# Second attention's running sums in fp32r, bias products merged, a new slot table for all stages

## The chip, the cores and the metric

One core of one Trainium2 chip runs the whole program. The metric is device time in microseconds of one launch. Engines are named as the profile names them: PE (TensorE), DVE (VectorE), ACT (ScalarE), POOL (GpSimd), SP (SyncE, here only a DMA queue).

## The reference

The input x is 2048 tokens of 128 numbers (8 sequences of 256). Six stages are added to it in turn, each on a layer-normed x:

```python
x = x + 0.5 * L0_ffn(_layernorm(x))     # 8 experts, top 2, hidden 256
x = x + L0_attn(_layernorm(x))          # silu projections, relu^2 of q k^T, gate
x = x + 0.5 * L0_ffn(_layernorm(x))
x = x + 0.5 * L1_ffn(_layernorm(x))     # 8 experts, top 2, hidden 352
x = x + L1_attn(_layernorm(x))          # linear attention, 16 heads
x = x + 0.5 * L1_ffn(_layernorm(x))
```

Each expert layer normalises once more (RMS), picks two of eight experts per token, and adds down(up * silu(gate)) by weight. The second attention, with phi = elu + 1, F = 4 features and G = 8 values per head, is

```python
kv = cumsum(einsum('bhtf,bhtg->bhtfg', K, V), axis=t)
Z = 1 / (einsum('bhtf,bhtf->bht', Q, cumsum(K, axis=t)) + 1e-6)
out = einsum('bhtf,bhtfg->bhtg', Q, kv) * Z
```

All values are fp32.

## The kernel before, in words

The tokens are split into four batches b of 512 (two sequences, four tiles of 128). The four expert layers are steps s = 0 to 3. In each, the two rows per token are sorted by expert with a scatter to `rows_dram`, so that a batch makes at most 15 tiles of 128 rows with one expert each. Thus there are 60 tiles a step and 240 in all, and tile n is slot n of one clock that all engines share: in slot t PE does `up(t)` (four products of 128x128 in steps 0 and 1, six in steps 2 and 3), then `down(t-2)` (two or three), then the transposes of a round of rows where one is due, then the stages of the chains. ACT does the silu of tile t, DVE the product `mult(t)`, SP loads weights four slots ahead. Every engine writes out its own list, slot by slot, and runs it in order; the slot is therefore not a time but a place in five queues, and semaphores tie them.

A chain (s, b) is what leads from the end of batch b's tiles in step s to its tiles in step s+1: POOL gathers the results (`gather`, eight indirect DMAs, offsets 2 to 5), DVE adds them (`combine`, in halves), attention follows in the chains s = 0 and 2, then routing (`route`) and the scatter (eight indirect DMAs on POOL). The offset of a stage is counted in slots from the end of the batch's tiles. The tables `COMBINE`, `ATTENTION` (stages j = 3 to 15 or 3 to 21) and `ROUTE` hold the offsets by hand. Chains of successive batches are 15 slots apart, so in a long middle stretch every slot holds stages of up to three chains. Chains s = -1 route the input: they begin `LEAD` slots before the batch's tiles, and slots from -30 on run before the first tile.

What ties PE to DVE: `up` has three banks `up_gate`, of which steps 2 and 3 use two per tile, so gate(n) needs mult(n-2) (`bank_free`), as does down(n-2). PE's small products share bank side2 in a fixed order of turns (`claim`).

Second attention, batch by batch, in banks side0 and side1: stage 7 transposes; 8 and 9 the q, k, v products with a bias product each (`ones_b` 3 rows times the split bias, bf16); 9 to 12 phi on DVE and ACT; 13 to 16 POOL makes k times v of tile t (`R[3 + t]`, 128x512); 14 the running sum of k (`tri`, and `ones` for the second tile of a sequence); 15 to 18 the running sums of kv; 15 DVE the denominator; 16 to 19 DVE multiplies by q and reduces; 20 transposes; 21 output product and bias. First attention has its own stages 7 to 15 with bias products in 9, 10 and 15.

## Time and profile before

| | us |
|---|---|
| median of 3 runs (659.34, 665.21, 665.27) | 665.21 |
| profiled execution | 665.68 |
| its span, first to last instruction | 664.0 |
| PE busy in it | 591.2 |
| DVE busy | 432.1 |
| ACT busy | 236.5 |
| POOL busy | 277.3 |
| mean granted clock of PE | 0.976 |

The span is 1.68 us shorter than the execution. PE's busy time is the union of its matmuls, with ends that are modelled; its weight loads run beside them. A row with "x8" is eight instructions of one kind merged. Every fp32 matmul shows as two records.

### The profile page before, as it was taken

What the parts mean: (1) busy time and instruction counts of PE and PEld (TensorE: products, weight loads), DVE (VectorE), ACT (ScalarE), POOL (GpSimd) and SP (SyncE); (2) the same over time, 40 slices, a digit from 0 to 9 for tenths busy, and PEclk for the clock granted to TensorE, in tenths of its full rate; (3) what the DMA queues carried; (4) which work ended last, traced back from release to release, by engine and by line L of the source; (5) the groups of instructions that cost most, each with busy time, mean ns of one, the idle gap of its engine ahead of it and who ended that gap; (6) DMA issues with size and microseconds to landing.
All of it is one profiled execution on the core that took longest, in us unless ns stands there. A gap on an engine that the chain in (4) does not pass through costs nothing.

```text
span 664.0 us, 15563 instructions
## 1 busy us (share of the span) xinstructions
PE 591.2 (89%) x4600; PEld 538.2 (81%) x4600; DVE 432.1 (65%) x1628; ACT 236.5 (36%) x466; POOL 277.3 (42%) x327
## 2 busy tenths in 40 slices
PE   1289989999999997899999999999999999998960
PEld 1179877989889797888999988988888889898960
DVE  4676582776768568657667739669869769572321
ACT  1034434353443433333433352342342343332320
POOL 2452636045170634573727182065075074170413
PEclk9999989999999999989999999999999999998995
DMA  8478869566665557588979876656765766777831
GB/s 297 172 234 229 282 186 278 146 184 192 194 178 171 166 173 220 168 260 248 305 222 282 224 228 168 178 164 171 194 159 167 197 176 174 216 209 241 240 86 43
DMA packets 114405, 133.18 MB, mean 201 GB/s; under 512 B 10931, under 2 KB 77491, under 8 KB 114070
## 3 DMA queue, kind: packets, MB, share of 16 engines
q1 hardware_dynamic: 106134, 115.39, 59.5%
q0 software_dynamic: 8192, 16.79, 8.6%
q8 instruction: 42, 0.69, 0.4%
q14 instruction: 37, 0.30, 0.1%
HBM read 103.05 MB, written 29.10 MB: 199 GB/s over the span
## 4 chain that ended last, share of the span: by engine, by line
PE 68%; DVE 14%; issue 6%; DMA 5%; POOL 4%; ACT 2%; SPq 1%; POOLq 0%; DVEq 0%; ACTq 0%
PE up_gate L907 19%; PE up_gate L900 13%; PE y L861 12%; PE side L915 3%; PE y L863 3%; POOL y_rows L456 2%; PE side L982 2%; PE side L931 2%; POOL rows_dram L440 2%; DVE hidden L591 2%; PE side L990 1%; PE side L999 1%; DVE x_res L641 1%; PE side L966 1%; DVE attn_xT L803 1%
## 5 line engine op out<-in xcount | busy, mean ns | idle before, releaser
L456 POOL DMA_INDIRECT y_rows<-y_dram,rows_of x128 | 128.9, 1007 | 250.6 <-DMA y_dram<-y_tile 216.1
L591 DVE TENSOR_TENSOR hidden<-up_gate,hidden 128x256 f32<-128x256 f32 (+1 forms) x240 | 116.6, 488 | 119.5 <-PE up_gate L907 58.8
L501 ACT ACTIVATE hidden<-up_gate 128x256 f32<-128x256 f32 (+1 forms) x240 | 104.6, 436 | 247.7 <-PE up_gate L907 125.9
L907 PE MATMUL up_gate<-rows_T,up 128*128 128x128 f32 x1440 | 184.9, 278 | 0.6 <-ACT hidden L501 0.4
L907 PEld LDWEIGHTS up_gate<-rows_T,up 128*128 128x128 f32 x1440 | 172.5, 193 | 9.0 <-issue 6.5
L440 POOL DMA_INDIRECT rows_dram<-rms_out,rows_of x128 | 127.4, 995 | 119.7 <-DVE rows_of L729 83.0
L900 PE MATMUL up_gate<-rows_T,up 128*128 128x128 f32 x960 | 135.8, 287 | 5.3 <-issue 4.0
L900 PEld LDWEIGHTS up_gate<-rows_T,up 128*128 128x128 f32 x960 | 122.6, 199 | 14.4 <-issue 11.0
L861 PE MATMUL y<-down,hidden 128*128 x480 | 75.3, 280 | 2.4 <-DVE hidden L591 2.3
L861 PE MATMUL y<-down_a,hidden 128*128 x480 | 73.7, 276 | 0.0
L861 PEld LDWEIGHTS y<-down,hidden 128*128 128x128 f32 x480 | 64.9, 196 | 3.0 <-issue 3.0
L861 PEld LDWEIGHTS y<-down_a,hidden 128*128 128x128 f32 x480 | 63.7, 193 | 0.0
L506 ACT ACTIVATE rows_T<-side,norm 128x512 f32<-128x512 f32 x64 | 42.2, 660 | 52.0 <-PE side L915 52.0
L494 ACT ACTIVATE y_tile<-y 128x512 f32<-128x512 f32 x64 | 36.5, 570 | 32.8 <-PE y L863 29.8
L863 PE MATMUL y<-down_b,hidden 96*128 x240 | 46.5, 275 | 0.0
L915 PE MATMUL side<-ident,rows 128*128 128x128 f32 x240 | 38.2, 280 | 7.0 <-DMA rows<-rows_dram 5.8
L863 PEld LDWEIGHTS y<-down_b,hidden 96*128 96x128 f32 x240 | 36.6, 192 | 0.0
L915 PEld LDWEIGHTS side<-ident,rows 128*128 128x128 f32 x240 | 29.0, 145 | 8.1 <-DMA rows<-rows_dram 8.0
L641 DVE SCALAR_TENSOR_TENSOR x_res<-y_rows,w_first,x_res 128x128 f32<-128x128 f32 x64 | 19.7, 350 | 22.9 <-DMA y_rows<-y_dram,rows_of 22.6
L926 PE MATMUL side<-ident,rms_out 128*128 128x128 f32 x64 | 10.8, 296 | 19.9 <-DVE rms_out L627 18.7
L926 PEld LDWEIGHTS side<-ident,rms_out 128*128 128x128 f32 x64 | 8.0, 151 | 20.1 <-issue 10.9
L931 PEld LDWEIGHTS side<-router,z_T 128*128 128x128 f32 x128 | 17.2, 209 | 6.5 <-ACT z_T L513 6.5
(159 smaller groups left out, 629.9 us busy)
## 6 DMA issues: line engine op xcount, KB each, us to landing
up<-in_up SPq DMA_DIRECT2D x120, 352.0 KB
up<-in_up SPq DMA_DIRECT2D x120, 256.0 KB
rows<-rows_dram SPq DMA_DIRECT2D x48, 256.0 KB, 3.6
y_dram<-y_tile SPq DMA_DIRECT2D x48, 256.0 KB
rows_dram<-zeros SPq DMA_DIRECT2D x12, 256.0 KB, 4.5
rows<-rows_dram SPq DMA_DIRECT2D x16, 192.0 KB
y_dram<-y_tile SPq DMA_DIRECT2D x16, 192.0 KB
rows_dram<-rms_out,rows_of POOLq DMA_INDIRECT x128, 3.2
```

Of the source, the lines that this page charges most:

```text
L440: pool.indirect_dma_start(out=xg_d[g], out_offset=bass.IndirectOffsetOnAxis(ap=pos[g][:, at:at + 1], axis=0), in_=xs(Z, GROUPS[g][c // TB] ...
L456: pool.indirect_dma_start(out=gath[b % 2][:, (TB * k2 + c) * P:(TB * k2 + c + 1) * P], out_offset=None, in_=y_d[g], in_offset=bass.Indirec ...
L494: act.activation(ysb[r % 4][:, 0:n * P], Y[r % 2][:, 0:n * P], ACT.Copy).then_inc(y_done, 1)
L501: act.activation(hid[n % 4][:, 0:w], src, ACT.Silu).then_inc(silu_done, 1)
L506: act.activation(xgT[r % 3][:, 0:n * P], S[2][:, 0:n * P], ACT.Copy, scale=wn[:, LAYER[s]:LAYER[s] + 1]).then_inc(s2_free, 1)
L591: dve.tensor_tensor(h, u, h, ALU.mult).then_inc(mult_done, 1)
L861: last = pe.matmul(y, hid[n % 4][:, c * P:(c + 1) * P], w, start=(c == 0), stop=(l == 0 and c == 1))
L863: last = pe.matmul(y, hid[n % 4][0:96, 2 * P:3 * P], dn1b[:, bass.ds(v * P, P)], start=False, stop=True)
L900: last = pe.matmul(U[q % 3][:, i * P:(i + 1) * P], upW[n % RING][:, at:at + P], rows_, start=True, stop=True)
L907: last = pe.matmul(U[q % 3][:, c * P:(c + 1) * P], upW[n % RING][:, at + c * P:at + (c + 1) * P], rows_, start=True, stop=True)
L915: last = pe.transpose(S[2][:, c * P:(c + 1) * P], xg[r % 4][:, c * P:(c + 1) * P], ident[:, :])
L931: last = pe.matmul(S[2][:, t * E:(t + 1) * E], zT[:, t * P:(t + 1) * P], wr[:, l * E:(l + 1) * E], start=True, stop=True)
```

## The change

Seven things change; the tables of slots with them.

1. ACT copies `tri` and `ones` once to fp32r. Per batch of the second attention ACT copies each kv tile to `kv_hi` (fp32r), DVE subtracts to get `kv_lo` (fp32r), and PE sums both: two fp32r products of 512 columns in place of one fp32 product.
2. PE's stages 15 to 18 now wait for `lo_ready` (DVE), DVE's stages 14 to 17 for `hi_ready` (ACT), ACT's stages 13 to 16 for `kv_ready` (POOL).
3. One bias product over a whole bank, ahead of the products that add to it: v and q, k, v from four to two per batch, both output products from four to one.
4. The running sum of k is one `tri` product of 256 columns and one `ones` product of 128 columns per batch, in place of six of 64.
5. The first load of a round's rows is issued one slot earlier (`LOAD_ROWS`).
6. `LEAD` rises by 5 and the table of step 0's routing with it, by differing amounts.
7. All offsets of `COMBINE`, `ATTENTION` and `ROUTE` are new. `LAG` has no effect (it is multiplied by 0 for groups of one batch).

```diff
-LOAD_ROWS = 2
-LEAD = 37
-
-COMBINE = (((7, 9),),
-           ((10, 10),),
-           ((6, 8),),
-           ((6, 9),))
-ATTENTION = (({3: 9, 4: 10, 5: 15, 6: 15, 7: 17, 8: 18, 9: 19, 10: 20, 11: 20, 12: 24, 13: 25, 14: 25, 15: 26},),
+LOAD_ROWS = 3
+LEAD = 42
+
+COMBINE = (((5, 10),),
+           ((10, 13),),
+           ((5, 9),),
+           ((7, 10),))
+ATTENTION = (({3: 10, 4: 12, 5: 12, 6: 12, 7: 14, 8: 15, 9: 16, 10: 17, 11: 18, 12: 19, 13: 19, 14: 19, 15: 20},),
-             ({3: 9, 4: 11, 5: 14, 6: 14, 7: 16, 8: 17, 9: 17, 10: 17, 11: 18, 12: 18, 13: 20, 14: 20, 15: 21, 16: 21, 17: 22, 18: 25, 19: 25, 20: 27, 21: 28},),
+             ({3: 10, 4: 13, 5: 13, 6: 15, 7: 17, 8: 18, 9: 18, 10: 18, 11: 19, 12: 19, 13: 21, 14: 22, 15: 23, 16: 24, 17: 25, 18: 27, 19: 27, 20: 29, 21: 29},),
-ROUTE = (({"stats": 7, "guess": 10, "root": 11, "norm": 12, "skip": 20, "z": 14, "score": 15, "first": 15, "second": 16, "rank": 18, "assign": 18, "weights": 20, "scatter": 19},),
-         ({"stats": 26, "guess": 27, "root": 28, "norm": 29, "skip": 31, "z": 31, "score": 33, "first": 34, "second": 34, "rank": 35, "assign": 35, "weights": 37, "scatter": 37},),
-         ({"stats": 13, "guess": 17, "root": 17, "norm": 18, "skip": 20, "z": 20, "score": 22, "first": 22, "second": 26, "rank": 27, "assign": 27, "weights": 35, "scatter": 29},),
-         ({"stats": 30, "guess": 30, "root": 31, "norm": 31, "skip": 40, "z": 33, "score": 33, "first": 33, "second": 33, "rank": 35, "assign": 35, "weights": 42, "scatter": 39},))
+ROUTE = (({"stats": 12, "guess": 12, "root": 12, "norm": 13, "skip": 17, "z": 16, "score": 17, "first": 17, "second": 18, "rank": 20, "assign": 20, "weights": 30, "scatter": 22},),
+         ({"stats": 21, "guess": 22, "root": 23, "norm": 26, "skip": 32, "z": 29, "score": 29, "first": 29, "second": 30, "rank": 31, "assign": 31, "weights": 31, "scatter": 31},),
+         ({"stats": 16, "guess": 18, "root": 19, "norm": 20, "skip": 21, "z": 22, "score": 23, "first": 23, "second": 25, "rank": 26, "assign": 26, "weights": 30, "scatter": 29},),
+         ({"stats": 30, "guess": 30, "root": 31, "norm": 31, "skip": 34, "z": 33, "score": 34, "first": 35, "second": 35, "rank": 36, "assign": 36, "weights": 48, "scatter": 40},))
...
+        kv_hi = [sb(f"kv_hi{i}", NT, F32R) for i in range(TB)]
+        kv_lo = [sb(f"kv_lo{i}", NT, F32R) for i in range(TB)]
+        tri_r = sb("tri_r", P, F32R)
+        ones_r = sb("ones_r", P, F32R)
...
                         act.wait_ge(min_ready, 2 * ka)
+                    if j in (13, 14, 15, 16):
+                        t = j - 13
+                        act.wait_ge(kv_ready, 4 * ka - 3 + t)
+                        act.activation(kv_hi[t][:, :], R[3 + t], ACT.Copy).then_inc(hi_ready, 1)
                     if j == 20:
                         act.wait_ge(attT_ready, ka)
...
             act.wait_ge(consts, 7)
+            act.activation(tri_r[:, :], tri[:, :], ACT.Copy)
+            act.activation(ones_r[:, :], ones[:, :], ACT.Copy).then_inc(const_pe, 1)
             act.wait_ge(norm_loaded, 32)
...
             def attention(l, s, j, b, ka):
+                if l == 1 and j in (14, 15, 16, 17):
+                    t = j - 14
+                    dve.wait_ge(hi_ready, 4 * ka - 3 + t)
+                    dve.tensor_tensor(kv_lo[t][:, :], R[3 + t], kv_hi[t][:, :].bitcast(F32), ALU.subtract).then_inc(lo_ready, 1)
                 if j == 3:
                 if j == 4:
...
                     if j in (9, 10):
                         pe.wait_ge(proj_used, 5 * ka - 3 + q)
+                        pe.matmul(tiles(S[1 - q][:, :], HID), ones_b[0:3, :], bias_v.unsqueeze(1).to_broadcast([3, 2, HID]), start=True, stop=False)
-                            o = S[1 - q][:, t * HID:(t + 1) * HID]
-                            pe.matmul(o, xT[:, (2 * q + t) * P:(2 * q + t + 1) * P], w_hid[:, 0:HID], start=True, stop=False)
-                            last = pe.matmul(o, ones_b[0:3, :], bias_v, start=False, stop=True)
+                            last = pe.matmul(S[1 - q][:, t * HID:(t + 1) * HID], xT[:, (2 * q + t) * P:(2 * q + t + 1) * P], w_hid[:, 0:HID], start=False, stop=(t == 1))
                     if j in (10, 11):
...
                     if j == 15:
                         pe.wait_ge(og_ready, 2 * ka)
+                        pe.matmul(tiles(S[1][:, :]), ones_b[0:3, :], bias_o0.unsqueeze(1).to_broadcast([3, TB, P]), start=True, stop=False)
-                            o = S[1][:, t * P:(t + 1) * P]
-                                pe.matmul(o, R[2 + c][:, t * P:(t + 1) * P], w_o0[:, c * P:(c + 1) * P], start=(c == 0), stop=False)
-                            last = pe.matmul(o, ones_b[0:3, :], bias_o0, start=False, stop=True)
+                                last = pe.matmul(S[1][:, t * P:(t + 1) * P], R[2 + c][:, t * P:(t + 1) * P], w_o0[:, c * P:(c + 1) * P], start=False, stop=(t == TB - 1 and c == 1))
                     if j in (8, 9):
                         pe.wait_ge(xT_ready, NB + ka)
+                        pe.matmul(tiles(S[q][:, :], 2 * P), ones_b[0:3, :], bias_qkv.unsqueeze(1).to_broadcast([3, 2, 2 * P]), start=True, stop=False)
-                            o = S[q][:, t * 2 * P:(t + 1) * 2 * P]
-                            pe.matmul(o, xT[:, (2 * q + t) * P:(2 * q + t + 1) * P], w_qkv[:, :], start=True, stop=False)
-                            last = pe.matmul(o, ones_b[0:3, :], bias_qkv, start=False, stop=True)
+                            last = pe.matmul(S[q][:, t * 2 * P:(t + 1) * 2 * P], xT[:, (2 * q + t) * P:(2 * q + t + 1) * P], w_qkv[:, :], start=False, stop=(t == 1))
                     if j == 14:
                         pe.wait_ge(phi_ready, ka)
-                        for t in range(TB):
-                            o = S[0][:, t * 64:(t + 1) * 64]
-                            last = pe.matmul(o, tri[:, :], R[0][:, t * P + 64:(t + 1) * P], start=True, stop=(t % 2 == 0))
-                            if t % 2:
-                                last = pe.matmul(o, ones[:, :], R[0][:, (t - 1) * P + 64:t * P], start=False, stop=True)
-                        last.then_inc(kcum_ready, 1)
+                        o = S[0][:, 0:TB * 64].rearrange("p (q t c) -> p t q c", t=2, c=64)
+                        k_of = R[0].rearrange("p (q t c) -> p t q c", t=2, c=P)
+                        pe.matmul(tiles(S[0][:, 0:TB * 64], 64), tri[:, :], tiles(R[0])[:, :, 64:P], start=True, stop=False)
+                        pe.matmul(o[:, 1], ones[:, :], k_of[:, 0, :, 64:P], start=False, stop=True).then_inc(kcum_ready, 1)
                     if j in (15, 16, 17, 18):
-                        pe.wait_ge(kv_ready, 4 * ka - 3 + t)
+                        pe.wait_ge(lo_ready, 4 * ka - 3 + t)
                             pe.wait_ge(v_ready, 2 * ka)
...
                             pe.wait_ge(cum_used, 4 * ka - 5 + t)
-                        last = pe.matmul(o, tri[:, :], R[3 + t], start=True, stop=(t % 2 == 0))
+                        pe.matmul(o, tri_r[:, :], kv_hi[t][:, :], start=True, stop=False)
+                        last = pe.matmul(o, tri_r[:, :], kv_lo[t][:, :], start=False, stop=(t % 2 == 0))
-                            last = pe.matmul(o, ones[:, :], R[2 + t], start=False, stop=True)
+                            pe.matmul(o, ones_r[:, :], kv_hi[t - 1][:, :], start=False, stop=False)
+                            last = pe.matmul(o, ones_r[:, :], kv_lo[t - 1][:, :], start=False, stop=True)
                     if j == 20:
                         pe.wait_ge(att_ready, ka)
...
                     if j == 21:
                         pe.wait_ge(attT_used, ka)
+                        pe.matmul(tiles(S[0][:, :]), ones_b[0:3, :], bias_o1.unsqueeze(1).to_broadcast([3, TB, P]), start=True, stop=False)
-                            o = S[0][:, t * P:(t + 1) * P]
-                            pe.matmul(o, R[1][:, t * P:(t + 1) * P], w_o1[:, :], start=True, stop=False)
-                            last = pe.matmul(o, ones_b[0:3, :], bias_o1, start=False, stop=True)
+                            last = pe.matmul(S[0][:, t * P:(t + 1) * P], R[1][:, t * P:(t + 1) * P], w_o1[:, :], start=False, stop=(t == TB - 1))
             def slot(t):
...
             pe.wait_ge(consts, 7)
-            pe.wait_ge(const_pe, 1)
+            pe.wait_ge(const_pe, 2)
             pe.wait_ge(norm_loaded, 32)
```

## Rows read from the trace of the kernel before

**Rows 1.** Part 1 of the page: busy us, share of the span, instructions.
```profile
PE 591.2 (89%) x4600; PEld 538.2 (81%) x4600; DVE 432.1 (65%) x1628; ACT 236.5 (36%) x466; POOL 277.3 (42%) x327
```

**Rows 2.** Busy time of PE, PEld, DVE, ACT, POOL in stretches; then clock, DMA share, GB/s.
```profile
99.00:252.00 153.00, 151.61 (x1082) 131.20 (x1082) 99.29 (x393) 63.55 (x129) 59.65 (x59) 1.00 0.65 188
...
252.00:312.00 60.00, 51.18 (x415) 48.52 (x414) 42.90 (x197) 22.63 (x49) 32.41 (x33) 0.94 0.74 221
...
384.00:572.00 188.00, 184.76 (x1399) 160.68 (x1398) 143.00 (x432) 70.41 (x129) 75.60 (x75) 1.00 0.65 181
```

**Rows 3.** The chain in order of time, 384 to 428 us: start, us, what.
```profile
387.03 0.63 PE side L999 x2
387.66 0.21 PE side L1000
...
397.05 0.45 PE side L1006 x4
...
400.22 1.72 PE side L1020 x4
...
421.03 0.42 PE side L1033 x2
421.45 0.16 PE side L1034
```

**Rows 4.** Groups of instructions by form, VectorE and ScalarE.
```profile
L767 DVE TENSOR_TENSOR attention<-attention 128x512 f32<-128x512 f32 x8 | 5.5, 692 | 7.5 <-ACT attention L537 7.5
...
L527 ACT ACTIVATE attn_xT<-side 128x512 f32<-128x512 f32 x4 | 2.4, 597 | 0.0
```

**Rows 5.** The same view, one period of the second attention.
```profile
460.28:508.67 48.39, 47.35 (x359) 41.08 (x358) 39.09 (x127) 18.05 (x34) 20.16 (x20) 1.00 0.64 175
```

**Rows 6.** What VectorE waited for in that period: us, times, longest.
```profile
DVE scores L684 <- PE side L931: 2.3, 1, 2.3
...
DVE x_res L810 <- PE side L1034: 1.1, 1, 1.1
```

**Rows 7.** Timeline of VectorE and GpSimd: start, us, what, idle before.
```profile
443.35 2.09 POOL L469 TENSOR_TENSOR attention<-attention 128x512 f32<-128x512 f32 x2 [3.29 <-DVE attention L785]
...
444.54 0.93 DVE L720 TENSOR_TENSOR_SCAN end_tile<-ones,n_tiles 128x8 f32<-128x8 f32 x1
...
447.96 2.10 POOL L469 TENSOR_TENSOR attention<-attention 128x512 f32<-128x512 f32 x2
...
448.58 1.54 DVE L793 TENSOR_SCALAR den<-den 128x64 f32<-128x64 f32 x1
```

**Rows 8.** Timeline of TensorE, 255 to 312 us.
```profile
261.85 0.19 PE L937 MATMUL side<-chosen,before_b 128*128 128x40 bf16 x1 [2.51 <-DVE chosen L699]
...
264.01 2.07 PE L900 MATMUL up_gate<-rows_T,up 128*128 128x128 f32 x8
...
278.37 1.15 PE L900 MATMUL up_gate<-rows_T,up 128*128 128x128 f32 x8 [0.36 <-DVE hidden L591]
...
289.24 0.66 PE L915 MATMUL side<-ident,rows 128*128 128x128 f32 x4 [1.55 <-DMA rows<-rows_dram]
```

**Rows 9.** Timeline around the first combine, 70 to 90 us.
```profile
71.67 1.05 POOL L456 DMA_INDIRECT y_rows<-y_dram,rows_of  x1 [1.09 <-DMA y_dram<-y_tile]
...
79.99 0.61 DVE L641 SCALAR_TENSOR_TENSOR x_res<-y_rows,w_first,x_res 128x128 f32<-128x128 f32 x2 [3.19 <-DMA y_rows<-y_dram,rows_of]
...
80.84 1.02 POOL L456 DMA_INDIRECT y_rows<-y_dram,rows_of  x1 [0.30 <-issue]
...
88.38 0.71 PE L861 MATMUL y<-down,hidden 128*128 x4 [1.59 <-DVE hidden L591]
```

**Rows 10.** Timeline of TensorE, a router product behind its transpose.
```profile
438.45 1.06 PE L931 MATMUL side<-router,z_T 128*128 128x8 f32 x8 [0.78 <-ACT z_T L513]
```

**Rows 11.** Timeline of VectorE at the start.
```profile
13.47 0.19 DVE L684 COPY scores<-side 128x32 f32<-128x32 f32 x1 [3.99 <-PE side L931]
...
19.34 1.25 DVE L680 TENSOR_SCALAR x_res<-x_res,b_skip_mul,b_skip_add 128x128 f32<-128x128 f32 x4
```

More of the change, by code:

```diff
@@ L65 @@
 ROWS_AT = 2
-LOAD_ROWS = 2
-LEAD = 37
-LAG = (4, 13, 6, 13, 5)
-COMBINE = (((7, 9),),
-           ((10, 10),),
-           ((6, 8),),
-           ((6, 9),))
-ATTENTION = (({3: 9, 4: 10, 5: 15, 6: 15, 7: 17, 8: 18, 9: 19, 10: 20, 11: 20, 12: 24, 13: 25, 14: 25, 15: 26},),
+LOAD_ROWS = 3
+LEAD = 42
+LAG = (0, 18, 21, 29, 6)
+COMBINE = (((5, 10),),
[3 more added lines that the diff above has]
+ATTENTION = (({3: 10, 4: 12, 5: 12, 6: 12, 7: 14, 8: 15, 9: 16, 10: 17, 11: 18, 12: 19, 13: 19, 14: 19, 15: 20},),
@@ L289, in macaron @@
         qkv_ready, min_ready, v_ready, exp_ready = sem("qkv_ready"), sem("min_ready"), sem("v_ready"), sem("exp_ready")
-        phi_ready, kv_ready, kcum_ready, den_used = sem("phi_ready"), sem("kv_ready"), sem("kcum_ready"), sem("den_used")
+        phi_ready, kv_ready, hi_ready, lo_ready, kcum_ready, den_used = sem("phi_ready"), sem("kv_ready"), sem("hi_ready"), sem("lo_ready"), sem("kcum_ready"), sem("den_used")
         cum_ready, cum_used = sem("cum_ready"), sem("cum_used")
```

## Prediction

> **What bounds the kernel now.** I read the page's first part, then busy time by stretch, then the chain, then who waited for whom, then the timeline of the places where PE sat idle. PE is busy for 591.2 of 664.0 us [rows 1], and by stretch for 151.61 of 153 us in the middle of the first layer and 184.76 of 188 us in the middle of the second [rows 2]. There the time is the sum of PE's records. Between them, at the end of step 1, it is not: 51.18 of 60 us, with a mean clock of 0.94 [rows 2]. So time can be won in two ways: by fewer matmuls in the two middles, or by closer order at the joint. DVE decides what can be kept: in a period of the second attention (15 tiles, 48.39 us) it is busy for 39.09 us [rows 5], and its waits come to 6.8 us in four rows, from 2.3 to 1.1 [rows 6]. The other 41.6 us it is tied up, the small gaps between linked operations included.
>
> **PE's savings.** An fp32 product of 512 columns takes 0.86 us (1.72 for four records, two products) [rows 3]. Six per batch, 5.16 us, become twelve fp32r products. No row shows that type. The nearest for one pass is a bf16 bias product of 256 columns, 0.21 us, and of 128 columns, 0.16 us [rows 3]; in a straight line 512 columns take 0.31, fixed cost included. The other bound is no speed-up at all, 0.86. In a chain of twelve alike the fixed part should be hidden, so I take 0.25: 3.0 us, 2.2 saved. At 0.21 it is 2.6; at 0.43 nothing; at 0.86 a loss of 5.2.
>
> A bias product of 256 columns costs its own 0.21 and makes the fp32 pair behind it 0.63 where two records without one take 0.43 (half of the 0.86 above, 256 columns for 512), so 0.41 [rows 3]. Two of the four in q, k, v go and two grow by 0.10: 0.6 saved. In the output product three of four go, each 0.16 and 0.20 (0.42 against 0.22), one grows by 0.15: 0.9. The running sum of k is 6 x 0.22 = 1.3 (0.45 for two products [rows 3]) and becomes 0.43 + 0.22: 0.65 saved. Second attention: 2.2 + 0.6 + 0.9 + 0.65 = 4.3 us per batch. First attention: 0.6 + 0.9 = 1.5. Over four batches that is 23 us of PE.
>
> **What DVE and ACT get.** The subtraction has the form of L767, 0.69 us, with its gap 0.72; the copy that of L527, 0.60 [rows 4]. Four of each per batch. ACT is busy for 18.05 of 48.39 us [rows 5], so 2.4 more is hidden, unless it waits: its stages 13 to 16 now wait for POOL, and behind them in its queue stand the silu of the next tiles, for which DVE's mult and then PE's banks wait. DVE goes from 41.6 to 44.5 us per period. PE goes from 48.4 to 44.1. Now DVE is the longer one. DVE's new waits for `hi_ready` have mult of the next tile behind them, and PE's for `lo_ready` have gate and up behind them.
>
> Neither can run ahead far: gate(n) needs mult(n-2). The new table puts combine, first, second, assign, all four subtractions, the denominator and two of the four q products at the period's slots 5 to 10, with PE's heavy slots (q, k, v, z) before them; second and rank are one slot apart where they were two. I allow 1.5 to 2 us for this: 46 to 46.5 us.
>
> **The hold on DVE.** POOL's kv products come in pairs of 2.1 us. A DVE scan over two SBUF inputs begun at 444.54 ended at 445.47 with POOL's pair (443.35 + 2.09), and a tensor_scalar begun at 448.58 ended at 450.12 with the next pair (447.96 + 2.10) [rows 7]. So DVE is let in only when the pair is over: together at most 2.4 us a period, of which I count 1.75 as loss. Before, gathers stood between the two pairs. Now stages 13 to 16 lie at offsets 21 to 24, behind all eight gathers of the next batch (offsets 2 to 5, that is 17 to 20), so the four products tend to run as one block of 4.2 us, or as two where ACT's v copy is late. In these slots DVE has first, second, assign and the subtractions, nearly all with two SBUF inputs. The hold may take 3 to 4.2 us, 2 more than now. That leaves 48 to 48.5 us in the periods of batches 1 to 3: no gain. Batch 0 has no routing of a batch before it beside it, so DVE is light and PE's 4 us arrive; batch 3 has no next batch's norm, and I give it 1. Second attention: -5 us.
>
> The Trainium skill, GPSIMD Engine Reference, Specifications, says that GpSimd shares its SBUF interfaces with VectorE and contends with instructions that run in a two-port mode or have two SBUF inputs. The two rows agree, one of each kind; by that rule every subtraction is exposed. Without it the periods would be 46 to 46.5 us and the sum some 6 us lower.
>
> **First attention.** PE saves 1.5 per batch. But z and score of the routing now share offset 29 (31 and 33 before): PE's score waits for ACT's copy of z. Where the second layer does this today, PE idles 0.78 us [rows 10]. Net 0.7 x 4 = -3 us. The shorter stages 8 to 15 bring offset 26 down to 20; by sums of the slots DVE has room (99.29 busy of 153 us [rows 2]). In the second layer z and score part, but stages 20 and 21 now share a slot, with ACT's copy between: these cancel.
>
> **Joint of steps 1 and 2.** The last batch's rank waited 2.51 us for DVE, behind which the clock fell (eight records 2.07 us against 1.15); a later rows load was 1.55 us late [rows 8]. In all 60 - 51.18 = 8.8 us idle, and clock 0.94 for 60 us, some 3.6 us lost [rows 2]. The new table ranks that batch at offset 31 instead of 35, four slots (of six products, each 0.22) or 5 us sooner, and apart from the next chain's z. The scatter behind it ends sooner too. The short waits (rank one slot behind second) stay. Of 12.4 us I take back 7; between 4 and 10. At the joint of steps 2 and 3 the scatter of the last batch stands on POOL behind the gathers of another, in the same order as before: nothing.
>
> **Start and first combine.** Step 0's routing moves `skip` of batch 0 ahead of its score, where DVE idled 3.99 us, and away from the path to batch 1 (1.25 us and two small operations) [rows 11], and weights too: -1.5 us. But the first batch's combine moves from offset 7 to 5. Its gathers cannot move: POOL starts at 71.67, after the stores, eight at 1.31 us until 80.84 [rows 9]. DVE already waited 3.19 us for the first half, until 79.99, and PE later 1.59 for DVE [rows 9]. Two slots (some 3 us) earlier, DVE waits 3 us longer with mult of the next tiles behind it, and PE, two tiles ahead at most, feels about 2 more. +2 us; between 0 and 5. For batch 0 of step 2 the same move by one slot of 2 us is hidden, since tiles there are longer (nine products for six). `LOAD_ROWS` puts SP's wait for the scatter one slot earlier, with weight loads behind it; these run four slots ahead, which hides it; without that cover it would cost PE one slot at each late scatter. The two constant copies on ACT lie under DVE's first statistics: nothing.
>
> **Sum,** against the profiled execution of 665.7 (median 665.2): -1.5 + 2 - 3 - 7 - 5 = -14.5, so 651 us.
>
> **Rivals.** (1) PE's savings arrive whole: DVE yields no time to POOL and its clumps fit. For it: PE, not DVE, ended nearly every wait before. Against: 44.5 against 44.1 us, and rows 7. Then second attention gives 17 to 20, first 4, joint 8 to 9, first combine +1: 665.7 - 32 = 634. Chance 0.22. (2) The hold grows into PE: rank waits 3.5 us in each of three periods and the clock falls to 1.2 GHz as behind the 2.51 us wait, about 2 us more each; the first combine costs 4. Second attention +2, joint -4: 665.7 - 1.5 + 4 - 3 - 4 + 2 = 663. Chance 0.18, a third of it over 665. (3) Slower: fp32r runs no faster per record than one fp32 record pair. Then the twelve products take 10.3 instead of 3.0 us in each batch, 7.3 x 4 = 29 more than I sum, and PE bounds again: 651 + 29 - 2 = 678. It decides from about 0.5 us a product, where the 14.5 us are gone if DVE's slack no longer hides it. No row excludes this; the bf16 rows, one record per product, only make it unlikely. Chance 0.06. That nothing changes on PE is excluded by the counts. The forecast itself: 0.54, own range 641 to 659.
>
> **Range and chances.** 0.8 of the chance lies between 634 (half of rival 1 below it) and 664 (most of rival 2 inside). Over 1% is what a measurement here can tell from no change: 658.5 and 671.8. Faster: forecast 0.5, rival 1 0.22, of rival 2 0.03, sum 0.75. Same: 0.17. Slower: rival 3 and the tail of rival 2, 0.08.
>
> **What would show it.** L1020's successor with 12 records per batch, step 0.21 to 0.31; second-attention periods of 46 to 48.5 us with DVE tied for over 44; PE waits for `chosen` (rank) or `kv_lo` that were not there; DVE operations beginning inside a block of POOL products and ending with it; a clock dip behind the longest of these; the stretch at the end of step 1 with under 5 us idle; DVE's first wait for y_rows at 6 us. I am wrong if the period is below 45 (then DVE's load was not binding), or if the joint keeps its 2.51 us wait, or if the first combine stops PE for over 5 us.

## The result and the profile after

| | before | after |
|---|---|---|
| median of 17 runs, us | 665.27 (659.34 to 667.64) | 657.91 (655.41 to 664.53) |
| ratio, 95% interval | | 0.9907 (0.9883 to 0.993) |
| profiled execution, its span | 665.68, 664.0 | 656.88, 655.1 |
| PE, DVE busy | 591.2, 432.1 | 572.6, 442.2 |
| mean granted clock | 0.976 | 0.970 |

The forecast was 651 (634 to 664), 14.5 us less. Direction and range held, the size did not: by the ratio the gain is 6.2 us (4.7 to 7.8), less than half. The profiled pair, on which the rest of this section stands, differs by 8.9 us in span, so 5.6 us of the 14.5 are missing in it.

To find where, I cut each span at the same tiles: a boundary is the start of the first gate and up product of a tile, read from PE's timeline. Columns are us, then the forecast and the measured difference to the kernel before. Each kernel has one profile; kernels with the same code in a stretch differ there by 1 to 2 us from one profile to the next.

| stretch | before | after | forecast | measured |
|---|---|---|---|---|
| start to tile 12 | 58.00 | 59.58 | -1.5 | +1.6 |
| 12 to 28: first combine | 31.17 | 31.25 | +2 | +0.1 |
| 28 to 88: first attention, four batches | 156.34 | 158.63 | -3 | +2.3 |
| 88 to 100: joint, with the last batch's rank | 26.74 | 23.89 | } -7 | -2.9 |
| 100 to 150: rest of the joint | 106.97 | 103.40 | } | -3.6 |
| 150 to 218: second attention | 209.67 | 205.12 | -5 | -4.5 |
| 218 to the end | 75.11 | 73.23 | 0 | -1.9 |

First attention misses its forecast by 5.3 us and the start by 3.1; the other stretches together came out 2.8 better than forecast.

The page's first part and the same stretches as [rows 1] and [rows 2]:

```profile
PE 572.6 (87%) x4528; PEld 534.1 (82%) x4528; DVE 442.2 (68%) x1644; ACT 245.0 (37%) x484; POOL 280.6 (43%) x327
```

```profile
99.00:252.00 153.00, 148.69 (x1053) 130.66 (x1052) 97.02 (x386) 62.91 (x127) 57.62 (x56) 0.98 0.61 180
252.00:312.00 60.00, 54.23 (x462) 51.15 (x461) 45.00 (x204) 24.79 (x55) 34.58 (x35) 1.00 0.82 248
384.00:572.00 188.00, 175.34 (x1392) 163.62 (x1391) 156.81 (x464) 80.86 (x150) 76.83 (x74) 0.98 0.64 184
```

PE has 18.6 us less work, and idles where it did not: in the first middle its busy share fell below that of before and the clock from 1.00 to 0.98; in the second, 12.7 us idle against 3.2. The joint improved: 5.8 us idle against 8.8, clock 1.00 against 0.94.

The new sums, timeline of PE (start, us, what). The step from one to the next is 0.23 us:

```profile
404.27 0.39 PE L1030 MATMUL side<-kv_lo,tri_r 128*128 128x512 f32 x1
404.50 0.40 PE L1032 MATMUL side<-kv_hi,ones_r 128*128 128x512 f32 x1
404.73 0.40 PE L1033 MATMUL side<-kv_lo,ones_r 128*128 128x512 f32 x1
404.97 1.50 PE L921 MATMUL up_gate<-rows_T,up 128*128 128x128 f32 x12
```

What stops PE most now, from its waits (us in total, times, longest), beside 16.9 us at the start (18.7 before):

```profile
PE side L951 <- DVE chosen L709: 12.8, 6, 3.0
PE side L929 <- DMA rows<-rows_dram: 8.2, 5, 2.6
PE side L945 <- ACT z_T L517: 4.7, 6, 0.8
PE y L875 <- DVE hidden L601: 4.3, 5, 2.1
```

**Second attention.** One choice operation over 32 columns takes 2.30 us and ends at 439.95 with POOL's pair, 0.05 later (POOL, then DVE, of the timeline); the add of 442.26 is stretched too. PE's rank waits behind them, in three batches alike, and in two the clock falls. That add is two records, and the second of them (442.53) ends at 443.69, behind the first product of POOL's next pair and while the second one runs; so it was let in between the two:

```profile
437.80 2.10 POOL L473 TENSOR_TENSOR attention<-attention 128x512 f32<-128x512 f32 x2
...
437.65 2.30 DVE L701 TENSOR_TENSOR picked<-is_max,pick 128x32 f32<-128x32 f32 x1
...
442.26 1.43 DVE L651 SCALAR_TENSOR_TENSOR x_res<-y_rows,w_second,x_res 128x128 f32<-128x128 f32 x2
...
442.53 1.16 DVE L651 SCALAR_TENSOR_TENSOR x_res<-y_rows,w_second,x_res 128x128 f32<-128x128 f32 x1
...
442.31 1.23 POOL L473 TENSOR_TENSOR attention<-attention 128x512 f32<-128x512 f32 x1 [2.42 <-ACT attention L549]
...
443.50 1.11 POOL L473 TENSOR_TENSOR attention<-attention 128x512 f32<-128x512 f32 x1
...
441.58 0.19 PE L951 MATMUL side<-chosen,before_b 128*128 128x40 bf16 x1 [2.11 <-DVE chosen L709]
...
489.10 0.21 PE L951 MATMUL side<-chosen,before_b 128*128 128x40 bf16 x1 [2.11 <-DVE chosen L709]
...
489.74 2.89 PE L921 MATMUL up_gate<-rows_T,up 128*128 128x128 f32 x12 [0.34 <-issue]
```

The last row, twelve records, takes 1.50 to 1.60 at 2.4 GHz; at 2.89 PE runs at 1.2.

**First attention.** Three short waits within 6 us, the 0.78 of [rows 10] among them, then two records at 1.92 us that take 1.02 at full clock:

```profile
168.25 0.71 PE L875 MATMUL y<-down,hidden 128*128 x4 [0.36 <-DVE hidden L601]
...
171.99 1.06 PE L945 MATMUL side<-router,z_T 128*128 128x8 f32 x8 [0.78 <-ACT z_T L517]
173.33 0.66 PE L964 MATMUL side<-ident,attention 128*128 128x128 f32 x4 [0.28 <-DVE attention L637]
...
175.99 1.92 PE L969 MATMUL side<-attn_xT,a_qk 128*128 128x512 f32 x2
```

DVE is late there since it had waited for gathered rows, which POOL had queued between scatters (DVE, then POOL):

```profile
165.49 0.61 DVE L651 SCALAR_TENSOR_TENSOR x_res<-y_rows,w_first,x_res 128x128 f32<-128x128 f32 x2 [0.99 <-DMA y_rows<-y_dram,rows_of]
...
142.10 1.02 POOL L444 DMA_INDIRECT rows_dram<-rms_out,rows_of  x1 [27.20 <-DVE rows_of L739]
...
147.28 1.05 POOL L460 DMA_INDIRECT y_rows<-y_dram,rows_of  x1 [0.30 <-issue]
148.63 1.00 POOL L460 DMA_INDIRECT y_rows<-y_dram,rows_of  x1 [0.31 <-issue]
149.94 1.35 POOL L444 DMA_INDIRECT rows_dram<-rms_out,rows_of  x1 [0.30 <-issue]
...
162.17 1.00 POOL L460 DMA_INDIRECT y_rows<-y_dram,rows_of  x1 [0.30 <-issue]
```

The kernel before had issued its eight gathers in one run, 140.43 to 150.61, with the eight scatters behind; now the sixteen are mixed and the last gather ends at 163.17.

**Joint, combine, start.** The 2.51 us wait of [rows 8] is 0.53, but rows from DRAM are late by 2.53 where they were by 1.27 or 1.55. The first combine's wait is 2.14 against 1.59 [rows 9]:

```profile
258.32 0.19 PE L951 MATMUL side<-chosen,before_b 128*128 128x40 bf16 x1 [0.53 <-DVE chosen L709]
...
282.34 0.65 PE L929 MATMUL side<-ident,rows 128*128 128x128 f32 x4 [2.53 <-DMA rows<-rows_dram]
...
82.40 0.81 PE L875 MATMUL y<-down,hidden 128*128 x4 [2.14 <-DVE hidden L601]
```

### The profile page after: what moved, and what is told of

Same layout as the page of the kernel before. It is cut to its first block, busy times and chain, and to the rows that moved or that the text cites. A ratio compares the mean times of both kernels' runs of the same rounds, so it can differ in the third digit from the quotient of the medians.

```text
span 655.1 us, 15452 instructions
## 1 busy us (share of the span) xinstructions
PE 572.6 (87%) x4528; PEld 534.1 (82%) x4528; DVE 442.2 (68%) x1644; ACT 245.0 (37%) x484; POOL 280.6 (43%) x327
## 4 chain that ended last, share of the span: by engine, by line
PE 61%; DVE 12%; issue 9%; POOL 7%; DMA 6%; ACT 2%; SPq 1%; POOLq 1%; DVEq 0%; ACTq 0%
PE up_gate L921 20%; PE y L875 11%; PE up_gate L914 11%; POOL rows_dram L444 4%; PE y L877 3%; PE side L929 3%; POOL y_rows L460 3%; DMA rows<-rows_dram 2%; DMA y_rows<-y_dram,rows_of 2%; DVE hidden L601 2%; DMA y_dram<-y_tile 1%; PE side L945 1%; DVE x_res L651 1%; DVE picked L701 1%; PE side L995 1%
## 5 line engine op out<-in xcount | busy, mean ns | idle before, releaser
L444 POOL DMA_INDIRECT rows_dram<-rms_out,rows_of x128 | 129.9, 1015 | 186.2 <-DVE rows_of L739 149.8
L875 PE MATMUL y<-down_a,hidden 128*128 x480 | 74.1, 277 | 0.0
L940 PE MATMUL side<-ident,rms_out 128*128 128x128 f32 x64 | 10.6, 292 | 16.9 <-DVE rms_out L637 16.9
L651 DVE SCALAR_TENSOR_TENSOR x_res<-y_rows,w_second,x_res 128x128 f32<-128x128 f32 x64 | 21.4, 376 | 1.1
```

The source lines that it names most:

```text
L444: pool.indirect_dma_start(out=xg_d[g], out_offset=bass.IndirectOffsetOnAxis(ap=pos[g][:, at:at + 1], axis=0), in_=xs(Z, GROUPS[g][c // TB] ...
L651: last = dve.scalar_tensor_tensor(xs(X, b, c * P, P), gath[b % 2][:, (TB * k2 + c) * P:(TB * k2 + c + 1) * P], wk[:, c:c + 1], xs(X, b, c ...
L875: last = pe.matmul(y, hid[n % 4][:, c * P:(c + 1) * P], w, start=(c == 0), stop=(l == 0 and c == 1))
```

## The experiments

Ratios are to the kernel before on the same chip (median there 662.5 to 665.05 for e5 to e18). Where a place is priced it is by the tile boundaries of the profiled run.

### Four on a chip where everything is slow

Here the kernel before took 825.84 us, and the four moved 158 to 165 GB/s where before and after moved 201 and 203 elsewhere, with waits all through the program. These runs say little of the other condition, and all four were repeated elsewhere.

e1, arithmetic of after, with LEAD, LOAD_ROWS and all tables of before:

```diff
-LOAD_ROWS = 3
-LEAD = 42
+LOAD_ROWS = 2
+LEAD = 37
 (COMBINE, ATTENTION, ROUTE as before)
```

> The new arithmetic (split sums, merged bias products, wide sum of k, the new waits) with the slot tables, LEAD and LOAD_ROWS of the kernel before. Theory A (the arithmetic carries the gain, the new slots of the first layer lose part of it): PE's 23 us less work arrive by about half, first layer -6 us with no new clock falls, second attention -4 to -8, in all -8 to -14 us, ratio 0.98 to 0.988, so faster than the change as a whole. Rival B (without slots made for it the split stalls: lo is late, DVE is overfull at offsets 20 to 22): second attention slower by 1 to 3 us a batch, in all -4 to +4 us, ratio 0.994 to 1.006, and the new slots were needed.

811.41 us, ratio 0.9847 (0.9782 to 0.9911).

e2, the reverse: tables, LEAD and LOAD_ROWS of after in the kernel before.

> The old arithmetic with the new tables, LEAD and LOAD_ROWS. Theory A: first layer loses 3 to 8 us to waits and clock falls, the joint of steps 1 and 2 gains 8, the second attention keeps 2.1 us rank waits: in all +2 to +8 us, ratio 1.003 to 1.012. Rival B (the new slots are where the gain comes from): -3 to -8 us, ratio 0.988 to 0.995.

844.98, 1.0273 (1.0224 to 1.0323).

e3, in the kernel after:

```diff
-... "norm": 26, "skip": 32, "z": 29, "score": 29 ...   (step 1)
+... "norm": 26, "skip": 32, "z": 27, "score": 29 ...
```

> The changed kernel with z of the routing behind first attention at offset 27 instead of 29, two slots ahead of score. Theory A (short waits that stack up bring the clock down): four waits of 0.78 us go, and with them the two falls of the clock at 175 and 216 us, 1.75 us each: -6.6 us against the change, ratio to the kernel before 0.980 to 0.982. Rival C (the falls belong to the other waits there, for mult and for the normalised rows): only -3 us, ratio 0.986, falls still there. Rival D (PE waits for z_ready instead): no change, 0.99.

827.75, 1.0052 (0.9994 to 1.011).

e4, the kernel after with `LEAD = 37` and step 0's row of ROUTE of before.

> The changed kernel with LEAD and the table of step 0's routing of the kernel before. In the change PE starts its tiles 0.43 us sooner and loses 2.0 us in tiles 2 to 12, with two waits for mult behind a DVE clump of statistics and Newton steps. Theory A (the clump costs it): the first waits go, tile 12 begins 1.5 us sooner, -1.5 us, ratio 0.988 to 0.989. Rival E (weight loads set the pace there, as DMA is busiest): no change, 0.990 to 0.991, tile 12 begins within 0.5 us.

831.11, 1.0125 (1.0064 to 1.0186). All that can be read here: on this chip the arithmetic alone gains and the new slots alone lose. The kernel after was not run on it.

### Arithmetic and slots apart (e5, e6)

e5 is e1's kernel again.

> The new arithmetic (fp32r sums, wide bias products, wide sums of keys) with all the old slots, LEAD and LOAD_ROWS. Theory A (the arithmetic carries the whole gain and the new slots give nothing on balance): 655 to 659 us, ratio 0.985 to 0.991; first attention's tiles 28 to 100 gain about 3 us here, because z stays two slots ahead of score, tiles 2 to 12 lose nothing, and the joint of steps 1 and 2 keeps its old 2.5 us waits. Rival B (the arithmetic needs the new slots): 661 to 666 us, because the second attention's period falls by less than 0.5 us per batch.

663.51, ratio 0.998 (0.9952 to 1.0009): rival B in size, but not for its reason. Periods of first attention are 37.33 against 38.83 us (tile 58 to 73): PE's 1.5 arrives whole, 7.4 us over tiles 12 to 100. Second attention is 7.0 us slower than before. There the new subtraction, one of 0.69 us alone, lies under POOL (DVE, POOL, PE):

```profile
391.70 3.18 DVE L763 TENSOR_TENSOR kv_lo<-attention,kv_hi 128x512 fp32r<-128x512 f32 x1
...
392.22 2.11 POOL L473 TENSOR_TENSOR attention<-attention 128x512 f32<-128x512 f32 x2
...
395.36 0.77 PE L1029 MATMUL side<-kv_hi,tri_r 128*128 128x512 f32 x1 [3.26 <-DVE k_den L804]
```

The profile puts PE's wait down to the operation right behind the subtraction; the subtraction ended 0.5 us before PE began.

e6 is e2's kernel again.

> The old arithmetic with all the new slots, LEAD and LOAD_ROWS. Theory A: 663 to 670 us, ratio 0.997 to 1.007, since the slots' gains (joint of steps 1 and 2, about -3.4 us, tail -1.4) are paid back by the start (+1.6) and by z in first attention. Rival B (the slots carry the gain): 657 to 661 us.

678.31, 1.0205 (1.0175 to 1.0234): neither theory. Second attention +13.8, first attention +3.8, start +1.6, joint -3.0. The largest single hold of the study stands here, two adds that take 0.61 us alone, the second of them held under four products in one block. By itself it took 4.90 us, from 400.49, and it began before the block did, while POOL still issued its last gather:

```profile
400.22 5.17 DVE L641 SCALAR_TENSOR_TENSOR x_res<-y_rows,w_second,x_res 128x128 f32<-128x128 f32 x2
...
401.08 4.14 POOL L469 TENSOR_TENSOR attention<-attention 128x512 f32<-128x512 f32 x4
```

So each half of the change alone is worth nothing or costs 14 us, and both together gain 6 to 7: the gain is neither's own.

### POOL's hold in the second attention (e7, e8, e17, e18)

e7, the kernel after:

```diff
-... "score": 34, "first": 35, "second": 35, "rank": 36 ...   (step 3)
+... "score": 34, "first": 34, "second": 34, "rank": 36 ...
```

> The kernel after with first choice of step 3's routing at offset 34 in place of 35 (second choice too), rank at 36. Theory A (the 2.1 us waits of PE for the chosen experts in batches 0 to 2 of the second attention, and the two falls of the clock behind them, are a cost of the routing's slots): the three rank waits fall below 0.5 us each, both clock falls at the end of the periods vanish, 649 to 653 us, ratio to the kernel before 0.977 to 0.983. Rival B (the second attention is limited by VectorE, whose work moves with it): the wait moves to another product and the time stays within 656 to 659 us.

657.46, 0.9899 (0.985 to 0.9949). The 2.1 us rank waits are gone, but `hidden` waits 2.19 us and `kv_lo` twice 1.14. Tiles 150 to 218: 204.9 against 205.1. Rival B.

e8, the kernel after with POOL's products over two heads of sixteen; the other fourteen are left out:

```diff
-  pool.tensor_tensor(R[3 + t] ... "p (h f g) -> p h f g" ..., kk ..., vv ..., ALU.mult)
+  pool.tensor_tensor(R[3 + t] ...[:, 0:2], kk ...[:, 0:2], vv ...[:, 0:2], ALU.mult)
```

> The kernel after, with POOL's products of keys and values cut to the first two heads of sixteen (64 of 512 columns; the rest of the products is left out, nothing else). Theory A (a VectorE operation that reads two arrays from SBUF is held by POOL's products until these end): the longest sub of routing (2.3 us), and the 1.4 us combine add, fall to about their own 0.7 us and 0.5 us; the rank waits of 2.1 us shrink to under 0.7 us, and the two falls of the clock in the second attention go, 5 to 9 us less than the kernel after beside it. Rival B (the rank waits come from the order of the routing's slots alone): the long operations shorten but the rank waits stay above 1.5 us, and the time changes by less than 3 us.

648.2 in one run. The choice operation takes 0.22 in place of 2.30 and rank waits 0.87, for ACT. Periods are 44.32 and 44.30 (DVE, then PE):

```profile
438.13 0.22 DVE L701 TENSOR_TENSOR picked<-is_max,pick 128x32 f32<-128x32 f32 x1
...
440.82 0.18 PE L951 MATMUL side<-chosen,before_b 128*128 128x40 bf16 x1 [0.87 <-ACT rows_T L510]
```

Tiles 150 to 218 take 194.7: with the hold gone the kernel after is 10.4 us shorter there. The cut also makes the products ready sooner, but in the kernel after only one wait there, of 0.9 us on ACT, was for them. And 44.3 is 4.1 below the 48.4 of before; against e18, which has the same cut, it is 3.4 below 47.7.

e17, the same cut in e5's kernel; e18, in the kernel before.

> The kernel of e5 (new arithmetic, old slots), with POOL's products of keys and values cut to 64 of 512 columns as in e8; the rest of these products is left out. In e5 tiles 150 to 218 took 7 us more than in the kernel before. Theory A (the old slots put the subtractions under POOL's pairs, which hold them and thus PE's sums): the 3.2 us subtraction and the 2.3 us weights operation fall to their own 0.7 and 0.2 us, PE's waits of 3.26 and 2.4 us before the second sum fall below 0.6 us, tiles 150 to 218 take 15 to 22 us less than in e5, 640 to 648 us. Rival B (these slots leave the sums too little room whatever POOL does): the waits stay above 1.5 us and the time above 655 us.

651.66, 0.9855 (0.9826 to 0.9884). Tiles 150 to 218: 203.7 against 216.7 in e5, 13.0 less (not all of it the hold: in e5 ACT waited 8.3 us for the products themselves, in e17 not at all); subtractions 0.69, PE's waits at most 0.76. Theory A by its mechanism; both its numbers were 2 to 4 us too hopeful, as these slots keep periods of 47.18 even so, where the new ones get 44.3.

> The kernel before with the same cut of POOL's products (the rest of them is left out). Theory A (before, the hold on VectorE cost nothing, because PE bound the periods with 47.35 us busy of 48.39): tiles 150 to 218 within 1.5 us of the kernel before, 663 to 666 us. Rival B (it already cost there): over 3 us less.

662.43, 0.9996 (0.9959 to 1.0034); tiles 150 to 218 -1.6, just outside theory A's 1.5 and not much over the spread between profiles. Before the change the hold cost next to nothing. It became dear when PE's cover of it went.

### What delays first attention (e9 to e11, e13, e14)

e9 is e3's kernel, e10 e4's, e11 has both edits.

> The kernel after with z of step 1's routing at offset 27 in place of 29, two slots ahead of score; nothing else changed. The old slots with the new arithmetic gave a first-attention period of 37.3 us where the kernel after has 38.2, 41.2 and 41.4, so the arithmetic did save its 1.5 us a batch. Theory A (PE's 0.78 us wait for z, beside two short waits for VectorE, costs itself and in batches 1 and 2 a fall of the clock): all three periods come to 37.3 to 37.9 us, no clock fall there, 8 to 9 us off, 648 to 651 us, ratio 0.975 to 0.98. Rival B (VectorE's operations of routing and attention in these slots bind, PE's wait is only where it shows): the wait moves to score, hidden or rank, periods 2 and 3 stay above 40 us, 655 to 658 us.

659.68, 0.9915 (0.9878 to 0.9953). The time is 1.7 us above rival B's range. My theory fell: the 0.78 us waits are gone, two periods are still 39.6 and 41.3, and PE now waits two slots earlier, for the input of z's transpose, and longer:

```profile
171.28 0.66 PE L940 MATMUL side<-ident,rms_out 128*128 128x128 f32 x4 [2.03 <-DVE rms_out L637]
```

> The kernel after with the old LEAD (37) and the old row of step 0's routing. Theory A (the new start puts statistics, guess and root of a batch in one slot, and VectorE's clump of them holds mult of the first tiles back): tiles 2 to 12 take 21.1 us again in place of 23.1, tile 2 starts at 36.9 in place of 36.4, 655.5 to 657 us, 1.5 us less than the kernel after. Rival B (the slots behind, tuned with the new start, lose by it): 658 to 661 us.

663.15, 0.9961 (0.9925 to 0.9996). The start to tile 12 is 57.7 again, as expected (59.6 in after), but tiles 12 to 100 lose 4.9 against after: the first combine at offset 5 now comes 1.8 us earlier, and PE waits 3.88 for what is behind it. The time is 2 us above rival B's 658 to 661, its reason is the one seen.

> Both edits: z at offset 27 and the old start, otherwise the kernel after. Theory A: the gains add, 646.5 to 649.5 us, ratio 0.972 to 0.978. Rival B (the clock falls elsewhere or VectorE binds in both): 653 to 658 us.

662.46, 0.9935 (0.9894 to 0.9976). Nothing adds; that is rival B's direction, 4 us above its range.

e13, the kernel after with four gathers in place of eight in step 0. The rows of each token's second expert are left out, and the combine adds the first row in their place (that edit is not shown):

```diff
-  for k2 in range(2):
+  for k2 in range(1 if s == 0 else 2):
-                    dve.wait_ge(gathered[b][h], 16 * TB * (s + 1))
+                    dve.wait_ge(gathered[b][h], 16 * TB * (s + 1) - 32)
```

> The kernel after, but in step 0 only the row of each token's first expert is gathered (four of eight indirect DMAs per batch; the first row is used in place of the second, which is left out). Theory A (with the new slots PE runs through the light slots at offsets 6 to 13 in 11 us, faster than POOL's eight gathers of 1.31 us and the landing of the last, so VectorE's combine waits 0.7 to 1.0 us for y_rows and all that stands behind it is late): VectorE's waits for y_rows in first attention vanish, and the periods of batches 1 and 2 fall from 41.3 to 38.2 us or less, 648 to 652 us. Rival B (it isn't the gathers but VectorE's own list, eight stages in the slots 10 to 14): VectorE's wait vanishes but the periods stay above 40 us, 653 to 657 us.

649.07, 0.9755 (0.9712 to 0.9798). Theory A: DVE's waits for y_rows in first attention are gone, three periods are 38.17 to 38.18, and the clock stays up:

```profile
170.18 1.06 PE L945 MATMUL side<-router,z_T 128*128 128x8 f32 x8 [0.78 <-ACT z_T L517]
...
173.00 1.02 PE L969 MATMUL side<-attn_xT,a_qk 128*128 128x512 f32 x2
```

Tiles 12 to 100: 206.4 against 213.8, of which 2.8 over tiles 12 to 28 and 4.6 over 28 to 88. With z's wait still there its price is some 38.18 - 37.33 (e5) = 0.85 a batch.

e14, the kernel after:

```diff
-ATTENTION = (({3: 10, 4: 12, 5: 12, 6: 12, 7: 14, 8: 15, ...
+ATTENTION = (({3: 10, 4: 11, 5: 13, 6: 13, 7: 15, 8: 15, ...
```

> The kernel after with first attention's stages 4, 5, 6 and 7 at offsets 11, 13, 13 and 15 in place of 12, 12, 12 and 14, so that VectorE has them in four slots in place of two. Theory A of the gathers: the wait for y_rows stays, the periods of batches 1 and 2 stay above 40 us, 655 to 659 us. Theory B of VectorE's list: the periods fall to 38 to 39 us, 650 to 654 us.

661.69, 0.9959 (0.9926 to 0.9992). The wait for y_rows stays (4.0 us in four), periods are 39.8, 41.5 and 43.1, the time 2.7 us above theory A's range: spreading DVE's list doesn't help.

### A better mixture (e12, e15, e16)

e12: the kernel after, so the new arithmetic, with the start, COMBINE and ATTENTION of step 0 and ROUTE of steps 0 and 1 as before; the rest as after, with e7's edit.

> The new arithmetic with the old slots for the start, the first chain (COMBINE, ATTENTION of step 0) and step 1's routing; the new slots for all that follows, with first and second choice of step 3's routing at 34. Theory A (each region is independent; each takes its better half): tiles 2 to 100 as with the old slots, 175.4 us from tile 2, 8.9 less than the kernel before; tiles 100 to 218 as with the new ones, 8 less; tail 2 less; 646 to 650 us. Rival B (the regions are tied: the old slots leave step 1's last batch late, and the new ones behind count on it early): tiles 100 to 120 lose over 3 us, 653 to 657 us.

653.35, ratio 0.983 (0.9794 to 0.9865), below the interval of the kernel after. The two weren't run side by side, so the some 5 us between them are a comparison through the kernel before. Tiles 12 to 100 are 206.3 (-7.9), 150 to 218 205.9 (-3.8). The joint keeps its late rank, and rows wait longer than in either kernel:

```profile
255.38 0.19 PE L951 MATMUL side<-chosen,before_b 128*128 128x40 bf16 x1 [2.21 <-DVE chosen L709]
...
275.03 1.12 PE L929 MATMUL side<-ident,rows 128*128 128x128 f32 x4 [3.77 <-DMA rows<-rows_dram]
```

e15 is e12 with first and second choice of step 1 at offset 33 (34 in e12).

> The kernel of e12 (old slots up to step 1's routing, new ones behind), with first and second choice of step 1's routing at offset 33 in place of 34, so that rank at 35 is two slots behind. Theory A (rank's 2.2 us wait at tile 95 and the clock after it are a matter of one slot): that wait falls below 0.6 us, 650 to 652 us. Rival B (VectorE is late there anyway and the wait moves to rows, which come from DRAM at tile 103): within 1 us of e12.

654.48, 0.983 (0.977 to 0.9891). Rank no longer waits over 0.6 us; PE waits 1.68 for `row_of` in its place, and 3.72 and 1.70 for rows. Rival B.

e16 is e12 without e7's edit.

> The kernel of e12 with first and second choice of step 3's routing at offset 35, as in the kernel after. Theory A (these offsets only move PE's wait in the second attention from rank to hidden and kv_lo): 2.1 us waits for chosen come back in three periods, those of 1.14 for kv_lo go, the time is within 1.5 us of e12. Rival B: 3 us or more slower than e12, since the clock falls behind the longer waits.

656.18, 0.9844 (0.9792 to 0.9897). The 2.1 us waits come back; the time can't be told from e12's.

## Why the prediction went wrong

**Reading of the bound: right for PE.** PE bounds both middles. What takes the gain back is in the second the hold on DVE, in the first the order of POOL's queue, which reaches PE through DVE.

**PE's savings: right.** 0.23 a product against 0.25 taken; per batch of the second attention PE's busy time at full clock fell from 47.35 to 43.37 us (e12), 4.0 against 4.3 forecast; 1.5 of the first against 1.5 (e5). Rival 3 is out.

**Second attention, -5: measured -4.5, in part by luck.** The hold is the named mechanism, and e8 and e18 show it by taking it away. Two of its terms were off and cancel. The hold was too small: without it I gave 6 us more, e8 gives 10.4, since two falls of the clock as in rival 2 came as well (the rank waits were 2.1, not 3.5). DVE's own load was too large: I called DVE the longer one and gave 46 to 46.5 us a period without the hold, e8 has 44.3, with PE busy for 42.4 of it. So DVE's load did not bind, only the hold did. And "let in only when the pair is over" was more than the rows said: the scan of 444.54 began beside the pair's second product, and in the kernel after the add of 442.53 was let in behind the first.

The Trainium skill, SBUF — State Buffer, SBUF: two separate sides, says that VectorE and GpSimd hold their shared port pair as an exclusive lock for the whole instruction, the other fully blocked. The rows agree with blocked. By this rule alone an operation would be let in between two products, some 1.07 us each: the add of 442.53 was, but in e6 DVE got in only behind the fourth, and at 439.95 in the kernel after behind the second. What decides between the two is open.

**First attention, "Net 0.7 x 4 = -3 us": wrong, the step that failed.** Tiles 28 to 88 took 2.3 us more instead of 3 less. The net's two terms hold: 1.5 saved, 0.85 for z against 0.78. I missed the third, a wait for POOL that I put at nothing. ROUTE's scatter of step 1 moves from offset 37 to 31, past the gathers of the batch two behind on POOL's queue (offsets 2 to 5, that is 32 to 35). In the prediction I asked of DVE only whether it had room (99.29 of 153 us [rows 2]) and took no account of POOL's order. The mixture makes the combine's rows late, DVE waits up to 1 us with mult behind it, and in two of three periods of steady work the clock falls: with the waits 3.05 us a period (41.23 - 38.18). That removing four gathers cures it is shown (e13: no wait for y_rows, no fall in the three periods of steady work, 4.6 us less over tiles 28 to 88). The order alone is not enough: e6 has the same mixture with the old arithmetic, its periods are 39.74, and DVE never waits for y_rows there. The shorter periods alone are not enough either: e5 and e12 have the old order, all eight gathers, periods of 37.3 to 37.7 and no such wait. As far as these runs go it takes both. That of all the slots it is the scatter's offset is read from the rows only: a kernel with just the scatter moved back was not tried.

**Joint, -7: right, -6.5.** 2.9 us came over tiles 88 to 100, where the rank wait fell by 2.0, and 3.6 over 100 to 150; the falls of the clock behind it are gone (252 to 312: clock 1.00). The rows load took 1 us back, and with 5.8 us idle the stretch missed my sign of under 5.

**Start, -1.5: wrong, +1.6.** The second batch's routing did end 1.8 us sooner (rank at 30.73 against 32.54), but PE then waited 2.58 us for rows from DRAM: 0.4 was left. I had not followed the rows behind the scatter. And over the first twelve tiles the new rows of slots cost 2.0 us, in which DVE runs statistics, variance, guess and root of one batch from 39.28 to 43.17 without a break; with the old start the twelve tiles take 20.9 us (e10), in after 23.2. I had priced what moves earlier and not what falls on the first tiles.

**First combine, +2: about right in size.** Tiles 12 to 28 changed by only +0.1 in the profiled pair, by luck of the pair: the seven profiles with the old slots there (before, e5, e12, e15 to e18) take 29.1 to 31.2 us, mean 30.4, after, e7, e8 and e9 with the new ones 31.3 to 32.6, mean 32.0. So the slots cost some 1.6. With half the gathers the same tiles take 28.5 (e13), so the combine waits for the gathers. The sign I gave, a first wait of DVE for y_rows of 6 us, did not come: it was 1.7.

**End, 0: wrong by 1.9.** Tiles 218 on took 73.23; e6, with the old arithmetic, has 73.17, so the new slots are enough for it. Which of them is open: e12, e15 and e16, with the new slots in steps 2 and 3 and the old ones before, have 74.1 to 74.4, and e5 with only the arithmetic 74.3.

## What to carry to other kernels

When a table of slots is moved, write down for every queue, that of GpSimd's DMAs too, the new order of what stands in it, before pricing any wait: sixteen indirect DMAs of 1.3 us don't care in which slot they are written, only behind what. An engine that bounds and gets lighter uncovers what it hid: taking GpSimd's hold on VectorE away was worth 1.6 us before and 10.4 after, so price the cover again after each saving. And test arithmetic and schedule apart and together: here apart they gave -0.2% and +2.1%, together -0.9%, and region by region -1.7%.

## What was not expected of the hardware

GpSimd's hold on a VectorE operation can outlast one product. An operation that began just before a block of products was held to the block's end: 0.19 us of work took 2.30 beside two (after, 437.65), and 0.35 us took 4.90 beside four (e6, 400.49). One that began beside the first product of a pair was in places let in behind it (after, 442.53) and in places not (before, 448.58, held until 450.12 by the pair of 447.96). What decides is not shown.

Behind three waits of PE of 0.36, 0.78 and 0.28 us the clock fell (after, first attention); in e13, where the 0.78 stood alone at the same place, it stayed.

And one kernel took 826 us on one chip and 662 to 665 on the others, 24% more, with 158 to 165 GB/s moved in the four runs profiled there.
